# Top-32 masks by two engines in turn, and scores made one item further ahead

## The reference

```
scores = jnp.einsum('bthd,bghd->bhtg', Q, K) / np.sqrt(DH)      # 4 heads, 1601 keys
topv, topi = jax.lax.top_k(scores, K_TOP)                       # K_TOP = 32
probs = jax.nn.softmax(topv, axis=-1)
attn = jnp.zeros_like(scores).at[bi, hi, ti, topi].set(probs)
attn_mean = attn.mean(axis=1)                                   # mean over the 4 heads
```

## Time and profile before

| what | value |
|---|---|
| median of 3 runs | 3124.41 us (3121.73 to 3128.46) |
| time of the profiled execution | 3121.85 us |
| its span | 3120.1 us |
| PE busy | 2426.9 us (78%) |
| DVE busy | 1525.3 us (49%) |
| ACT busy | 1423.9 us (46%) |
| POOL busy | 930.0 us (30%) |
| mean granted clock of PE | 0.874 of 2.4 GHz |

### The profile page before, as it was taken

How to read it: one execution, slowest core, us unless ns; L and a number is a source line. 1 busy time by engine, 2 the same in 40 slices (tenths; PEclk the granted TensorE clock), 3 DMA queues, 4 the chain that set the end, 5 groups by cost and what they waited for, 6 DMA issues and landing times.

```text
span 3120.1 us, 37524 instructions
## 1 busy us (share of the span) xinstructions
PE 2426.9 (78%) x13244; PEld 1460.9 (47%) x13244; DVE 1525.3 (49%) x4261; ACT 1423.9 (46%) x2266; POOL 930.0 (30%) x411
## 2 busy tenths in 40 slices
PE   0565798989965996669798669798769798769898
PEld 0532222222223664456475456476446476346466
DVE  8655002121231111985743894833795733795742
ACT  3043576676841222651364651264561264561264
POOL 1023000100001113560380470390570290460191
PEclk9987898999987998679898679899669999669999
DMA  1054643334151111002111103021103021002021
GB/s 58 1 195 147 132 57 72 50 66 66 48 190 28 46 45 36 30 8 105 27 33 34 35 8 105 25 31 37 34 3 110 21 35 37 28 1 105 0 31 38
DMA packets 176808, 168.41 MB, mean 54 GB/s; under 512 B 84064, under 2 KB 147168, under 8 KB 176576
## 3 DMA queue, kind: packets, MB, share of 16 engines
q1 hardware_dynamic: 169088, 156.36, 19.8%
q0 software_dynamic: 7504, 9.35, 1.6%
HBM read 133.52 MB, written 32.32 MB: 53 GB/s over the span
## 4 chain that ended last, share of the span: by engine, by line
PE 56%; DVE 21%; issue 9%; ACT 7%; DMA 4%; SPq 1%; POOL 1%; DVEq 0%; ACTq 0%; POOLq 0%
PE ps L1661 7%; PE ps L1271 5%; PE ps L1282 4%; PE ps L1646 4%; PE ps L1672 4%; DVE sb_xnT L2271 4%; ACT sb_arena L937 3%; PE ps L1538 3%; PE ps L1439 2%; PE ps L1608 2%; PE ps L1458 2%; PE ps L1452 2%; PE ps L1506 2%; PE ps L1588 2%; PE ps L1597 2%
## 5 line engine op out<-in xcount | busy, mean ns | idle before, releaser
L937 ACT ACTIVATE sb_arena<-ps 128x1024 f32<-128x1024 f32 x416 | 402.9, 1021 | 172.6 <-PE ps L1271 163.0
L2412 DVE TENSOR_REDUCE sb_arena<-ps 128x2 f32<-128x1024 f32 x128 | 156.4, 1224 | 271.4 <-PE ps L1672 270.6
L2271 DVE MAX8 sb_xnT<-sb_arena 128x8 f32<-128x60 f32 (+1 forms) x1728 | 245.8, 203 | 80.4 <-ACT sb_arena L1031 80.4
L1271 PE MATMUL ps<-sb_arena 96*128 96x512 bf16 x832 | 239.9, 395 | 53.2 <-issue 33.7
L1661 PE MATMUL ps<-sb_arena 128*128 128x64 f32 x2048 | 242.3, 272 | 0.0
L826 POOL TENSOR_TENSOR sb_arena<-sb_arena 128x1601 f32<-128x1601 f32 x56 | 175.5, 3133 | 217.2 <-DVE sb_arena L2259 217.2
L1661 PEld LDWEIGHTS ps<-sb_arena 128*128 128x128 f32 x2048 | 238.4, 192 | 0.0
L1282 PE MATMUL ps<-sb_arena 128*32 128x512 f32 x1664 | 227.2, 619 | 1.4 <-ACT sb_arena L937 1.4
L1519 PE MATMUL ps<-sb_arena,sb_ones_col 128*1 128x128 bf16 (+1 forms) x832 | 86.4, 284 | 181.0 <-DVE sb_arena L2301 126.3
L1109 ACT ACTIVATE sb_arena<-ps 128x512 f32<-128x512 f32 x256 | 151.7, 593 | 143.9 <-PE ps L1646 143.9
L763 POOL DMA_INDIRECT taken_rows<-sb_taken,sb_slots x32 | 31.3, 978 | 598.5 <-DVEq L2039 590.0
(11 more groups left out here) (340 smaller groups left out, 4568.9 us busy)
## 6 DMA issues: line engine op xcount, KB each, us to landing
sb_arena<-in_ctxT SPq DMA_DIRECT2D x13, 1601.0 KB, 7.3
sb_arena<-k_spill SPq DMA_DIRECT2D x96, 208.0 KB, 8.1
sb_arena<-in_dft SPq DMA_DIRECT2D x5, 2048.0 KB, 7.7
k_spill<-sb_arena SPq DMA_DIRECT2D x12, 832.0 KB, 5.2
sb_arena<-in_w SPq DMA_DIRECT2D x16, 512.0 KB, 6.5
sb_arena<-in_idft SPq DMA_DIRECT2D x4, 2048.0 KB, 8.4
sb_arena<-in_wf SPq DMA_DIRECT2D x8, 1024.0 KB, 11.5
o_rows<-sb_arena SPq DMA_DIRECT2D x32, 256.0 KB, 2.3
```

Of the source, the lines that this page charges most:

```text
L937: A(probs0[:, 2 * (m % 4):2 * (m % 4) + 2, :], ps[:, 2 * (m % 2):2 * (m % 2) + 2, :], ACT.Exp).then_inc(pair_probs, 1)
L1271: ins = mm(ps[:, 2 * (m % 2) + i, :], k_stack[0:NSPLIT, h, k * P:(k + 1) * P], q_stack[0:NSPLIT, h, :], start=True, stop=True)
L2271: ins = V.max(cand[:, n % 2, 8 * j:8 * j + 8], s_sb[:, n % 6, c0:c0 + w])
```

## The change

1. The mask of odd items is made by ACT instead of DVE, as the Sign of score minus a bound just under the 32nd largest. It is then +1 and -1 instead of 1 and 0; the copy in `scale_head` becomes a Relu, which turns the unwanted negative products into 0, and the expected count becomes one number for even items and another for odd ones.
2. DVE computes that bound in three more instructions on one column, one of which waits for the others, before it releases ACT.
3. The mask of even items stays on DVE, and its instruction also accumulates the number of kept keys of each row. The Sign does so too. `count` is now one matmul of one column instead of 13 pieces of 128.
4. ACT takes the exponential of the 32 ahead of the count, and its copy of the count no longer accumulates.
5. `settle` for an odd item is done at k == 6 instead of k == 4.
6. PE makes `scores(n + 4)` in item n instead of `scores(n + 3)`; `scores(3)` goes among the value projections ahead of item 0. `score_out(n + 3)` stays where it is on ACT.

```diff
-ALL_DECIDED = int(np.float32(P * TOPK).view(np.int32))
+ALL_DECIDED = [int(np.float32(P * n).view(np.int32)) for n in (TOPK, GKEYS - 2 * TOPK)]
+JUST_UNDER = 2.0 ** -22
...
                     pool.wait_ge(e1_ready, nth(b, e1_ready, n + 1))
+                    if n % 2:
+                        pool.wait_ge(sign_ready, nth(b, sign_ready, n // 2 + 1))
...
-                    A(p if n % H1 else p_mean[:, t % 2, 0:GKEYS], p, ACT.Copy, scale=stat1[:, n % 3, WEIGHT:WEIGHT + 1]).then_inc(p1_scaled, 1)
+                    A(p if n % H1 else p_mean[:, t % 2, 0:GKEYS], p, ACT.Relu, scale=stat1[:, n % 3, WEIGHT:WEIGHT + 1]).then_inc(p1_scaled, 1)
...
                     A(probs1[:, n % 3, 0:GKEYS], s_sb[:, n % 6, 0:GKEYS], ACT.Exp, bias=bias).then_inc(e1_ready, 1)
-                    act.wait_ge(count_done, nth(b, count_done, n + 1))
-                    A(kept_by_col[0:1, :], ps[0:1, 7, 3 * P:4 * P], ACT.Copy, accum_out=kept[0:1, n:n + 1]).then_inc(count_ready, 1)
+                    if n % 2:
+                        if n >= 3:
+                            act.wait_ge(count_done, nth(b, count_done, n - 1))
+                            act.wait_ge(p1_kept, nth(b, p1_kept, n - 1))
+                        A(kept01[:, 1, 0:GKEYS], s_sb[:, n % 6, 0:GKEYS], ACT.Sign, bias=under[:, 2:3], accum_out=kept_by_row[:, 1, :]).then_inc(sign_ready, 1)
                     A(top_e[:, n % 2, :], top[:, n % 2, :], ACT.Exp, bias=bias,
                       accum_out=stat1[:, n % 3, SUM:SUM + 1]).then_inc(sum1_ready, 1)
+                    act.wait_ge(count_done, nth(b, count_done, n + 1))
+                    A(kept[0:1, n:n + 1], ps[0:1, 7, 3 * P:3 * P + 1], ACT.Copy, scale=-1.0 if n % 2 else 1.0).then_inc(count_ready, 1)
...
-                    pe.wait_ge(choice_ready, nth(b, choice_ready, n + 1))
+                    if n % 2:
+                        pe.wait_ge(sign_ready, nth(b, sign_ready, n // 2 + 1))
+                    else:
+                        pe.wait_ge(choice_ready, nth(b, choice_ready, n // 2 + 1))
                     if n >= 1:
                         pe.wait_ge(count_ready, nth(b, count_ready, n))
-                    for i in range(KCH):
-                        k = -i % KCH
-                        ins = mm(ps[0:1, 7, 3 * P:3 * P + KW[k]], ones_col[:, :], kept01[:, n % 2, k * P:k * P + KW[k]],
-                                 start=(i == 0), stop=(i == KCH - 1))
+                    ins = mm(ps[0:1, 7, 3 * P:3 * P + 1], kept_by_row[:, n % 2, :], ones[:, :], start=True, stop=True)
...
-                    if n - len(COLS) in (0, 2, 4):
+                    if n - len(COLS) in (0, 2, 4, 6):
                         scores((n - len(COLS)) // 2)
...
-                    if n + 3 < TILES * H1:
-                        scores(n + 3)
+                    if n + 4 < TILES * H1:
+                        scores(n + 4)
...
-                        if k == 4 and n >= 1:
+                        if k == (6 if (n - 1) % 2 else 4) and n >= 1:
                             settle(n - 1)
                             weight(n - 1)
...
-                    V.tensor_scalar(st[:, NEG:NEG + 1], eights[:, 0:1], -1.0, None, ALU.mult).then_inc(top_ready, 1)
-                    if n >= 2:
-                        dve.wait_ge(p1_kept, nth(b, p1_kept, n - 1))
-
-                    V.tensor_scalar(kept01[:, n % 2, 0:GKEYS], s, eights[:, TOPK - 1:TOPK], None, ALU.is_ge).then_inc(choice_ready, 1)
+                    least = eights[:, TOPK - 1:TOPK]
+                    if n % 2:
+                        if n >= 3:
+                            dve.wait_ge(sign_ready, nth(b, sign_ready, n // 2))
+                        V.tensor_scalar(st[:, NEG:NEG + 1], eights[:, 0:1], -1.0, None, ALU.mult)
+                        V.tensor_scalar(under[:, 0:1], least, JUST_UNDER - 1.0, 1.0e-30, ALU.mult, ALU.add)
+                        link(V.tensor_scalar(under[:, 1:2], least, -1.0 - JUST_UNDER, None, ALU.mult))
+                        V.tensor_scalar(under[:, 2:3], under[:, 1:2], under[:, 0:1], None, ALU.max).then_inc(top_ready, 1)
+                    else:
+                        V.tensor_scalar(st[:, NEG:NEG + 1], eights[:, 0:1], -1.0, None, ALU.mult).then_inc(top_ready, 1)
+                        if n >= 2:
+                            dve.wait_ge(p1_kept, nth(b, p1_kept, n - 1))
+                            dve.wait_ge(count_done, nth(b, count_done, n - 1))
+
+                        V.tensor_scalar(kept01[:, 0, 0:GKEYS], s, least, 0.0, ALU.is_ge, ALU.add, accum_out=kept_by_row[:, 0, :]).then_inc(choice_ready, 1)
```

More of the change, by code:

```diff
@@ L134, in program @@
         ones_row = sb("ones_row", [P, P], BF16)
-        ones_col = sb("ones_col", [P, 1], BF16)
         norms = sb("norms", [P, 4])
@@ L246, in program @@
         kept01 = at(o, [2, KS], BF16); o += KS
-        kept_by_col = at(o, [P]); o += P
+        kept_by_row = at(o, [2, 1]); o += 2
+        under = at(o, [3]); o += 3
         probs1 = at(o, [3, KS]); o += 3 * KS
@@ L452, in program @@
         sum1_ready = sem("sum1_ready", 16)
-        choice_ready = sem("choice_ready", 16)
+        choice_ready = sem("choice_ready", 8)
+        sign_ready = sem("sign_ready", 8)
         count_ready = sem("count_ready", 16)
@@ L1725, in setup_program @@
                 link(V.memset(ones_row[:, :], 1.0))
-                link(V.memset(ones_col[:, :], 1.0))
                 link(V.memset(every[:, :], 1.0))
@@ L2237, in settle @@
                     kept_bits = dve.value_load(kept[0:1, n:n + 1].bitcast(I32), min_val=0, max_val=2 ** 31 - 1)
-                    with dve.If(kept_bits != ALL_DECIDED):
+                    with dve.If(kept_bits != ALL_DECIDED[n % 2]):
                         dve.wait_ge(e1_ready, nth(b, e1_ready, n + 1))
@@ L2309, in _ @@
                     dve.wait_ge(e1_ready, nth(b, e1_ready, n + 1))
-                    link(V.scalar_tensor_tensor(s_cut[:, 0:GKEYS], kept01[:, n % 2, 0:GKEYS], stat1[:, n % 3, WEIGHT:WEIGHT + 1],
-                                                probs1[:, n % 3, 0:GKEYS], ALU.mult, ALU.mult))
+                    link(V.scalar_tensor_tensor(s_cut[:, 0:GKEYS], kept01[:, n % 2, 0:GKEYS], 0.0, probs1[:, n % 3, 0:GKEYS], ALU.max, ALU.mult))
                     dve.wait_ge(p1_added, nth(b, p1_added, n - TILES))
-                    V.tensor_tensor(mean, mean, s_cut[:, 0:GKEYS], ALU.add).then_inc(p1_added, 1)
+                    V.scalar_tensor_tensor(mean, s_cut[:, 0:GKEYS], stat1[:, n % 3, WEIGHT:WEIGHT + 1], mean, ALU.mult, ALU.add).then_inc(p1_added, 1)
                 dve.wait_ge(p1_added, nth(b, p1_added, TILES * (H1 - 1)))
```

## The result

The changed kernel takes 3140.26 us (median of 5 runs, 3139.48 to 3141.53), the kernel before 3122.52 us beside it (5 runs, 3121.64 to 3128.46): a ratio of 1.0059, interval 1.0048 to 1.0071. It is slower by 0.6%, where I forecast 3095 us and a range up to 3120.

The account below looks back on a forecast made before the run. DVE bounded a plain item at 8.12 us; afterwards the ring (7.2) and DVE (7.13) would be level. Four batches gaining 7.2 us give 29, so 3093 from 3121.85; with 2.6 for the median, 3095, range 3045 to 3120.

Parts of the forecast that it names:

- item 8: Top-32 stage: high-clock scores and the second context product stand ahead of the count; forecast 9.3 us.
- the odd turn: Plain odd item: 7.2 us, with exponential, Sign and exponential of the 32 hidden beside the scores (3.45 against 3.75).
- DVE's side: DVE's work in the stage: odd item 6.34 us, even 7.91, a pair 14.25, 7.13 per item against 8.12.
- The ring: ACT and PE in turn, nothing overlapping: copy-out, scores, count, its copy, scale_head; 7.2 us per plain item.
- The even turn: Plain even item from copy-out through scores, count, its copy and scale_head: 7.2 us.
- item 6: 12 transposes between scores and count (2.8 us) and attn_turned copies (1.6) added to 7.2: 11.6 us.
- rival 2: Low clock in context items too, a context product about 6.3 us: slower, 3167 us; chance 0.08.
- The last items: DVE sets the pace from item 14: 7.91 us, then about 3.8 for item 15; last count at 2331.1, before 2338.3.
- Rival 1: DVE binds throughout because PE gets the high clock in plain items (ring 5.4 us): 3049 us; chance 0.20.
- Rival 3: Gain and new waits cancel: each ring turn 0.5 us longer, 6 us per batch: 3119 us; chance 0.12.
- Rival 4: On ACT, Sign needs another table than the exponential, two 1.28 us loads per odd item: 3167 us; chance 0.03.
- The signs to look for: Stage: no long odd masks on DVE, ACT's count waits behind scores, DVE idle 2 to 3 us at settle (7, 9, 11).

Follow-up runs that it names:

- e3_bound: The changed kernel with the unused ones_col allocated again and the bound's margin halved to 2**-23: 3108.75 us, 0.9973 of the kernel before.
- e8_count: The kernel before with accumulating masks on DVE for all items and the one-column count, nothing else: 3092.29 us, ratio 0.9921.
- e7_products: e3_bound with scale_head before the count's copy in even items, transposes and second context product behind the count, their copies one item later: 3062.79 us, 0.9824.

## Why the prediction was wrong, step by step

The forecast was a change of -29 us; the medians differ by +17.7, the two spans by +19.6. The gap of 48 us in the spans divides, by the table of stretches, into 18 for the redo, 18 for the rest of the table's second line (11 gained in four batches instead of 29; in the stage itself some 13.5), and 13 for stretches outside it (7.8 + 8.0 - 3.1). Without the redo and with the arena in place the gain is still only 8.5 us (e3_bound), so the terms of the stage failed too, and item 8 and the odd turn below are where.

- **The redo was in no term and no rival.** I described the new bound as "just under the 32nd largest" and priced its three instructions, but never asked what else it lets through, and what the branch behind the count costs when it is taken. Whether it is taken hangs on the data: one row in 4 x 4 x 512 has two scores that are 3.75e-7 apart. Before, the same count came out as expected 64 times of 64. A step that turns an exact comparison into one with a margin and keeps a fallback should have been a rival at 18.8 us per case; the rows for its price stood in the trace (an instruction of DVE on 1601 columns takes about 1.88 us, and the body has ten of them; measured, nine take 1.8 and the mask 0.99, with small ones between).
- **The arena was in no term.** I read the removal of `ones_col` as nothing. It moved every address behind it. What it costs is a later landing of `o_rows`, 1.2 us, and products behind it at a lower clock, 1 us, about 2 us per stretch. Of the 13 us outside the stage, 8 lie between the batches: about 2 in each stretch for that, and the rest is the granted clock's, which made the third stretch before (286.5) and the first after (290.2) faster than their neighbours; of the 7.8 ahead of the first keys, up to 6 are the spread of one kernel (1212.5 us in the kernel after, 1206.5 in its repeat).
- **DVE's side held.** Even mask 1.87 us, as taken, three small instructions 0.3 us (2238.75 to 2239.04), odd item without its mask. In items 2 and 3 DVE is idle for only 0.65 of 14.8 us, so its 14.25 for a pair is right within 0.1. All 64 masks of e8_count, 1868 to 1883 ns beside POOL or not, agree with the sentence of the Trainium skill, "SBUF — State Buffer", section "Who interferes with whom", that I had weighed.
- **The ring held in kind.** The even turn is 7.0 us (7.2), item 6 11.35 (11.6), items 7 and 9 7.0 and 7.3 (7.2). The odd turn was mis-sized: 7.8, not 7.2. I had the exponential and the Sign "hidden beside the scores"; but the exponential waits 1.22 us for DVE's bound (L2312), and the Sign then ends 0.75 us after the scores. Behind it is a step that I priced at nothing: from ACT's copy of the even count (2234.99) to DVE's first instruction behind the branch (2236.33) 1.3 us pass, in which DVE loads a register, compares and jumps, and 0.65 us of it DVE stands idle.
- **Item 8 was mis-sized**, 11.25 us for 9.3. The first context product took 5.92 us for the 3.7 that I took from rows of before. This is the mechanism of rival 2 in one of the two products: it ran at a granted clock of 0.50 from end to end, and the second at 1.00 in 3.17 us, as predicted. So half of rival 2 was true, and I had given it 0.08, because the clock rose inside the product before. A pause ahead of it doesn't explain the difference: PE had idled 4.06 us ahead of item 7's scores in the kernel after, and 4.19 us ahead of its count in the kernel before. Why the clock came back later here is open.
- **The last items** lost another 1.3 us. In all the third batch's last count ended 3.1 us earlier, counted from its first exponential, instead of 7.2: 0.9 lost until item 2, 0.8 in four plain items, 1.2 to item 12, 1.3 behind it.
- **Rivals.** Rival 1 is what e7_products almost reaches (3062.79 for 3049), by another cause: not a higher clock in plain items, but less work inside the ring. Rival 3, 0.5 us more per turn or 6 us per batch, is near the 4.1 that the third batch lost against the forecast, and named neither its place nor the item. Rival 4 is wrong: no table load stands between exponential and Sign.
- **The signs to look for** were all there (odd items without a long mask, waits for the count behind scores, DVE waiting 3.12 us for the count of item 6, ACT 4.84 and 6.07), and the time still was outside the range. They told of the stage alone.

What stays open: the size of the arena's effect on the whole time, why the clock came back later in item 7's product, and by how much the chip's scores of that one row miss or meet the bound.

## What to carry to other kernels

A branch on data that "never" runs is a term of the sum as soon as a change loosens its condition; look up the closest case in the data and price the body. When two in-order engines hand work back and forth, write down the whole turn, and keep everything that is not in it (here transposes and a context product) behind the hand-over: the same work, moved by a few lines, made 38 us. And look where a removed tensor stood: what is allocated behind it moves.

## What the runs showed of the hardware

- The accumulating mask over 1601 fp32 columns takes 1.87 us (1868 to 1883 ns in 64) and 0.08 us for the read, whether POOL works or not; the plain one 1.04 to 3.63 us. With it and the one-column count the kernel was 27 us faster (e8_count).
- A Sign over 1601 columns takes 1.62 us and 0.19 for its accumulator, and no table load stands between it and the exponential in any of the eight kernels that have it; each batch has one, 1.3 us ahead of its first exponential.
- From a 1x1 copy on ACT to the first DVE instruction behind a register load and a branch: 1.0 to 1.4 us where DVE waited for it in items 0 to 13 of the kernel after (1.34 in item 2, 2234.99 to 2236.33; 1.04 in item 6, 2267.38 to 2268.42).
- With the arena 224 bytes behind a multiple of 256, the same DMA packets took 21.1 to 21.2% of the engines' span, and 19.6 to 20.5% with it on one; PE's wait for `o_rows` grew from 8.4 to 9.4 us to 9.8 to 10.7.
- A wait that grew by 1.2 us cost 2.3: the products behind it took 6.2 us instead of 5.2, at a mean granted clock of 0.60 instead of 0.73.
